# Grouped feed-forward: when the expert weights are split into a high and a low part

## The reference, cut to what matters

```python
scores = softmax(x @ gate_w.T)               # 16 experts
topk_w, topk_idx = top_k(scores, 4)
topk_w = topk_w / sum(topk_w)
cw = zeros((T, E)).at[arange(T)[:, None], topk_idx].add(topk_w)
def _mlp(x, wg, wu, wd):
    return silu(x @ wg.T) * (x @ wu.T) @ wd.T
for each expert e:  acc += cw[:, e] * _mlp(x, w_gate[e], w_up[e], w_down[e])   # width 176
y = acc + _mlp(x, sw_gate, sw_up, sw_down)                                      # shared, width 352
```

## Time and profile before

| what | us |
|---|---|
| median of the runs | 1494.38 |
| the profiled execution | 1495.86 |
| its span | 1494.1 |
| TensorE busy / VectorE busy / ScalarE busy / GpSimd busy | 1313.7 / 1039.1 / 851.1 / 849.9 |
| TensorE's granted clock, mean over the span | 0.949 |

### The profile page before, as it was taken

One profiled execution on the slowest core, in us unless ns is written; L12 is line 12 of the kernel. 1 busy time (PEld: TensorE's weight loads), 2 busy tenths in 40 slices (PEclk: granted clock), 3 DMA queues, 4 the chain that ended last, 5 costly groups with the idle time before them and its releaser, 6 DMA issues.

```text
span 1494.1 us, 28548 instructions
## 1 busy us (share of the span) xinstructions
PE 1313.7 (88%) x8106; PEld 1102.4 (74%) x8106; DVE 1039.1 (70%) x2544; ACT 851.1 (57%) x2102; POOL 849.9 (57%) x752
## 2 busy tenths in 40 slices
PE   6999999999978986759898999899999989978983
PEld 4888888888867974547777777677777769867882
DVE  5676666656677545338888888788888877677545
ACT  1444444454435542248787877677778875435542
POOL 3555555530424773257877878677877740434772
PEclk9999999999988998759999999999999999979996
DMA  3000000002334336121222222122221202335335
GB/s 116 26 26 27 26 25 25 16 18 63 122 127 155 104 101 225 46 53 33 64 58 70 48 68 60 46 52 68 61 58 44 57 1 77 121 117 169 103 103 184
DMA packets 52271, 110.72 MB, mean 74 GB/s; under 512 B 11616, under 2 KB 21408, under 8 KB 51872
## 3 DMA queue, kind: packets, MB, share of 16 engines
q1 hardware_dynamic: 40992, 82.22, 19.2%
q0 software_dynamic: 9024, 24.65, 5.4%
q10 hardware_dynamic: 2112, 2.10, 0.4%
HBM read 64.11 MB, written 15.47 MB: 53 GB/s over the span
## 4 chain that ended last, share of the span: by engine, by line
PE 38%; issue 21%; POOL 19%; DVE 12%; DMA 5%; ACT 3%; POOLq 0%; SPq 0%; DVEq 0%; ACTq 0%
PE ps L1465 25%; PE ps L1620 7%; POOL pb_odd L1105 4%; POOL yt L1105 3%; DMA raw_w<-in_wx 3%; PE ps L1830 2%; POOL rb L1090 2%; DVE rb L547 2%; POOL z L1105 2%; DVE x_res L858 2%; POOL pb_low L1105 2%; POOL xg L1044 1%; POOL ra L1094 1%; PE ps L1552 1%; POOL ybuf L1053 1%
## 5 line engine op out<-in xcount | busy, mean ns | idle before, releaser
L917 DVE TENSOR_TENSOR pt_lo<-ps,pt_hi 128x512 fp32r<-128x512 f32 (+3 forms) x384 | 205.4, 548 | 53.3 <-ACT pt_hi L1384 47.0
L1465 PE MATMUL ps<-kh,qh 128*128 128x512 f32 (+3 forms) x768 | 203.8, 375 | 20.7 <-DMA qh<-qt_hi 9.0
L1384 ACT CAST pt_hi<-ps 128x512 fp32r<-128x512 f32 (+3 forms) x384 | 178.5, 481 | 58.8 <-PE ps L1830 51.1
L902 DVE TENSOR_REDUCE nmb<-ps 128x1 f32<-128x1024 f32 (+7 forms) x256 | 191.7, 749 | 27.2 <-PE ps L1465 26.1
L1465 PEld LDWEIGHTS ps<-kh,qh 128*128 128x128 f32 x768 | 131.7, 195 | 43.7 <-issue 12.6
L1465 PE MATMUL ps<-pt_hi,vst 128*128 128x512 f32 (+3 forms) x384 | 156.0, 406 | 1.2 <-DVE ra L882 1.1
L1044 POOL DMA_INDIRECT xg<-zbuf,gidx x94 | 97.5, 1037 | 101.3 <-DVE sidx L762 30.3
L1465 PE MATMUL ps<-pt_lo,vst 128*128 128x512 f32 (+3 forms) x384 | 132.3, 348 | 0.0
L1182 ACT ACTIVATE pa<-sma,nmax 128x192 f32<-128x192 f32 x128 | 57.3, 449 | 129.4 <-DVE nmax L584 105.2
L1009 POOL TENSOR_TENSOR pa<-pa,rinv 128x384 f32<-128x384 f32 x64 | 52.9, 827 | 130.5 <-DVE rinv L592 130.5
L1465 PE MATMUL ps<-w_ex,gx_hi 128*128 x376 | 103.2, 357 | 18.5 <-issue 16.9
(11 more groups left out here) (225 smaller groups left out, 4168.2 us busy)
## 6 DMA issues: line engine op xcount, KB each, us to landing
raw_w<-in_wx SPq DMA_DIRECT2D x36, 608.0 KB, 4.0
rb<-raw SPq DMA_DIRECT2D x192, 64.0 KB, 2.0
yg<-ybuf SPq DMA_DIRECT2D x8, 1024.0 KB, 8.2
qh<-qt_hi SPq DMA_DIRECT2D x64, 128.0 KB, 2.3
qh<-qt_lo SPq DMA_DIRECT2D x64, 128.0 KB, 2.4
wa<-in_wa SPq DMA_DIRECT2D x16, 384.0 KB, 3.0
wb<-in_wb SPq DMA_DIRECT2D x8, 384.0 KB, 3.7
wo_a<-in_wo_a SPq DMA_DIRECT2D x16, 128.0 KB, 2.0
```

The source lines that it names most:

```text
L902: v.tensor_reduce(nmb[:, par, i:i + 1], ps[:, b:b + 2, :].rearrange("p b k -> p (b k)")[:, 0:P * (t + 1)], AX.X, ALU.max, negate=True).the ...
L917: v.tensor_tensor(pt_lo[:, s % 3, at], ps[:, 4 + s % 2, at], pt_hi[:, s % 3, at].bitcast(F32), ALU.subtract).then_inc(sem("b_pt_lo"), 1)
L1384: s_.copy(pt_hi[:, s % 3, at], ps[:, 4 + s % 2, at]).then_inc(sem("b_pt_hi"), 1)
L1465: return t_.matmul(o, l, r, start=start, stop=stop)
```

## The change

Only the two tables change. Before, two weights are converted in three steps: high part of one, then high part of the next together with the remainder of the first, then the remainder of the next. After, one weight is converted in two steps: its high part at the end of an even step on ScalarE, its remainder at the end of the odd step behind it on VectorE. Steps 0 to 3 stay.

```diff
-ACT_HI = {0: (2,), 1: (3,), 2: (4,), 3: (5,), 5: (6,), 7: (7,), 9: (8,), 10: (9,), 12: (10,), 13: (11,), 15: (12,), 16: (13,),
-          18: (14,), 19: (15,), 22: (16,), 23: (17,)}
-DVE_LO = {7: (6,), 8: (7,), 10: (8,), 11: (9,), 13: (10,), 14: (11,), 16: (12,), 17: (13,), 19: (14,), 20: (15,), 23: (16,), 24: (17,)}
+ACT_HI = {0: (2,), 1: (3,), 2: (4,), 3: (5,)}
+ACT_HI.update({6 + 2 * (n - POOL_LO): (n,) for n in range(POOL_LO, N_W)})
+DVE_LO = {7 + 2 * (n - POOL_LO): (n,) for n in range(POOL_LO, N_W)}
```

## The result

The changed kernel takes 1488.74 us (median of 8 runs, 1482.41 to 1492.39) beside 1494.95 for the kernel before (8 runs, 1490.80 to 1497.09): ratio 0.9953, 95% interval [0.9937, 0.9969]. Forecast: 1484, range 1479.5 to 1490.5. The change does what was said, and is worth about 7 us by the ratio (4.6 to 9.4 by its interval; the medians differ by 6.2), not 10.8.

A forecast was written before the change was run, and what follows sets the result against it. Each layer was paced by the routing table, then the split's load waits, then GpSimd; gains of 6.1 us in f and 4.7 in g, together 10.8, led from the runs' median to 1484 us, range 1479.5 to 1490.5.

The forecast's parts named there:

- the load wait: ScalarE's waits for raw weights in both feed-forward layers: 28.9 us before, forecast to fall under 17.
- one stall: Mixed stretch, TensorE at position 18: the only stall per four-step cycle, 1.3 us, behind a remainder on VectorE.
- the late weight: Weight 17's remainder, now in step 29, delays position 31's gate/up products: 2.4 us once per layer, bounds 0 and 3.3.
- GpSimd carries: Behind b=17, GpSimd's pace of 2.57 us per gather carries the gain to each layer's end.
- rival A: Part given back through a dearer routed stretch and last remainder, or TensorE's clock: gain 3 to 8 us, about 1489; chance 0.28.
- routed stretch: Steps 22 to 29 cost more than before: 5.46 us per weight against 4.24, bounds 5.15 and 6.2.
- b=17: GpSimd's gather of iteration 17, first behind the last remainder: forecast about 6 us earlier in f, 5 in g.
- first weights: Start of the split, up to G(15): 2.1 us earlier in f, 1.9 in g.
- G(15): TensorE's start of the gate/up products for position 15: forecast at 447.1 in f, 1343.8 in g.
- mixed stretch: Four-step cycle from G(15): forecast 9.3 us, against 12.4 in f and 11.7 in g before.
- tie with TensorE: At b=17 GpSimd's own path takes 36.1 us, TensorE's 36.25, so meeting remainders costs nothing.
- held gathers: GpSimd's dense stretch: four gathers per layer meet a remainder, taking 1.77 us instead of 0.97, 0.8 more each.

The follow-up runs named there:

- e10: The changed kernel once more, unaltered, on one chip with e11: 1488.79 us, 0.9954 of the kernel before.
- e2: Kernel before (old order), loading only the first quarter of each raw weight from number 8 on: 1483.69 us, 0.9922 of the kernel before.
- e3: Changed kernel, loading only the first quarter of each raw weight from number 8 on: 1487.11 us, 0.9934 of the kernel before.
- e5: Changed kernel, each remainder's large instruction taking its first input from PSUM instead of the raw weight: 1487.58 us, 0.9949 of the kernel before.
- e6: Changed kernel with both e4's order and e5's PSUM input: 1481.49 us, 0.9912 of the kernel before.
- e9: Changed kernel with indirect scatters replaced by plain SyncE stores, GpSimd only gathering: 1472.46 us, 0.985 of the kernel before.
- e4: Changed kernel with weights 14 to 17 in pairs again (high parts in steps 22, 23, 25, 26): 1486.19 us, 0.9939 of the kernel before.
- e1: The changed kernel again, no edit: 1487.22 us, 0.9948 of the kernel before.
- e8: Kernel before (old order) with indirect scatters replaced by plain SyncE stores, GpSimd only gathering: 1479.32 us, 0.9892 of the kernel before.
- e7: Changed kernel with weights 6 to 8 converted in steps 5 to 7, last remainder in step 25: 1483.34 us, 0.9919 of the kernel before.
- e11: e7's order once more, unaltered, on one chip with e10: 1482.58 us, 0.9922 of the kernel before.

## Why the prediction was right, and where its size was off

The time, 1488.74, lies inside the range, and the mechanism is the one forecast: the load wait goes, one stall is left, the late weight costs, GpSimd carries. But the gain, 6 to 7 us, is below the forecast's own band of 8 to 13.5 and in that of rival A, 3 to 8, whose two causes (a dearer routed stretch, TensorE's clock) both turned up in part. Of the signs named, the one on b=17, about 6 and 5 us earlier, failed in size: it was 3.9 and 4.0.

Each term as forecast and as measured, us gained, from the layer's first gather:

| term | forecast | after | e10 |
|---|---|---|---|
| first weights, f: G(15) | 2.1 | 0.5 | 0.5 |
| first weights, g | 1.9 | 2.1 | 2.2 |
| mixed stretch, f: G(15) to G(19) | 3.1 | 3.2 | 3.2 |
| mixed stretch, g | 2.4 | 2.5 | 2.5 |
| G(19) to b=17, f | 0.9 | 0.2 | 0.2 |
| G(19) to b=17, g | 0.4 | -0.6 | -0.2 |
| sum at b=17 | 10.8 | 7.8 | 8.3 |
| sum at the end | 10.8 | 6.4 | 7.8 |

**The load wait and the mixed stretch: right.** Walked 9.3, measured 9.22 in both layers, with the one stall at position 18 where it was put (in f X(19) 6.37 after G(15) for 6.3, G(18) 7.34 for 7.25). The waits for raw weights fell to 14.4 us, below the 17 named. e2 shows the cause: short loads alone bring the old order to 9.4.

**First weights: right in g, a quarter in f.** This is the largest miss, 1.6 us. In the profiles after, TensorE is granted the lower of its two levels (1.2 instead of 2.4 GHz) in f's first positions behind the first gather; before, it was not. Busy time and granted clock (the column behind the five engines) of 430 to 440 us, before and then after, and of 460 to 470 after, which answers to the earlier trace rows:

```profile
430.00:440.00 10.00, 6.80 (x46) 6.11 (x46) 6.50 (x17) 4.26 (x10) 5.35 (x6) 0.99 0.64 201
```

```profile
430.00:440.00 10.00, 7.61 (x35) 6.64 (x34) 5.22 (x15) 3.48 (x8) 6.08 (x6) 0.67 0.46 142
...
460.00:470.00 10.00, 9.17 (x62) 8.00 (x61) 7.96 (x21) 6.58 (x17) 5.34 (x5) 1.00 0.61 196
```

35 instructions in 7.61 us of busy time, where before 46 took 6.80. G(10), a pair of products that takes 0.58 at the full clock:

```profile
436.79 0.95 PE L1465 MATMUL ps<-w_ex,gx_hi 128*128 x2 [0.47 <-issue]
```

From G(10) to G(12) it takes 5.4 us in f, and 3.7 in g, where the full clock is back 6 us behind the first gather, just before G(10). Over the profiles of the new order, unaltered or with one edit, G(15) of f goes with the moment at which the granted clock is back at the higher level, both in us from the first gather: back at 6.0 to 6.4, G(15) at 17.6 to 18.5 (e3, e5, e6, e9); back at 8.9 and 9.1, G(15) at 19.4 and 19.1 (e4, e1); back at 10.9 and 11.6, G(15) at 19.8 and 19.9 (the first profile after, e10). My walk assumed 2.4 GHz throughout and put it at 18.2. So the clock is what the term left out, though no run changes the clock alone. Why it is late in f is open. In the old order it is back at 1.3 and 1.6 (before, e2) but at 8.9 in e8, so the lower clock isn't the new order's doing alone; in all ten profiles that spread the conversions (e7 and e11 too) it is back only at 6.0 or later. Whether the new order makes it likelier, so few profiles don't tell. The lower clock that I had named for 460 to 470 (rival A) is gone there, as the walk said.

**The routed stretch and weight 17: right in kind, 0.7 and 1.1 us too short.** In f, G(19) to G(24) is 12.95 for 12.7, G(24) to G(30) 16.57 for 16.4, G(30) to G(31) 4.90 for 4.6; X(33) and the gather follow in 1.89 and 0.65 as walked: 36.96 for 36.25. In g one place is worse: G(24) to G(26) takes 5.82 instead of 5.5, with an idle of 0.91 (5.48 in e10, so not in every execution). Here rival A was partly true, at a quarter to a third of the 3.1 per layer given for it. In e1, e3 and e5 the idle 2.7 ahead of G(31) is followed by products at the lower clock (0.93 to 0.95 us for a pair that takes 0.58): the clock's share of rival A exists, but not in every execution.

**GpSimd: the pace right, its tie with TensorE right in kind, the size and number of held gathers wrong.** I took 1.77 for each of four; there are nine long ones per layer, of 1.31 to 1.73, so 0.3 to 0.8 more each; of those from b=8 on in f, five, none is over 1.41, and they sum to 1.9 for the 3.2 of my walk. The trace says why they are shorter. b=8 of f starts at 469.04, when this remainder has run for 0.6 us:

```profile
468.44 1.15 DVE L768 TENSOR_TENSOR w_ex<-raw_w,w_ex 128x960 fp32r<-128x960 f32 x1
```

Each long gather or scatter ends some 0.84 us after the remainder it met, so what it loses is what was left of the remainder: with 0.2 us gone it takes 1.77, as before, and with 0.6 gone 1.4. One that had started before the remainder isn't held (1.00 us for the scatters of f that do). That this is the remainder's doing was read from the trace, and e5 shows it: with one input in PSUM all nine are gone. The Trainium skill, page "SBUF — State Buffer", section "Who interferes with whom", has a rule that fits this, that a VectorE instruction with two SBUF inputs contends with a GpSimd instruction that reads SBUF, and one with at most one SBUF input, outside the two-port modes, doesn't. The same section's inference that a tensor_tensor leaves descriptor generation alone doesn't hold in these runs. That it "costs nothing" in the new order is right as well, to within what e5 can tell. The cover is thin: GpSimd was ready 1.54 us before TensorE in f and 0.25 in g, where the walk had 0.15, and in g it is that thin only by the gap ahead of iteration 9, which the walk didn't have.

**Behind b=17: 1:1, less up to 0.8 per layer.** The sum at the end is 0.5 to 1.4 below that at b=17. From b=17 to the last gather it takes 64.2 us in both layers, before and after, so up to there nothing is lost. Behind it the last block's gate and up products start 7.7 / 6.8 after the last gather before, 8.5 / 7.7 after and 8.0 / 7.1 in e10; in f TensorE stands 1.30 there for gathered rows to land, where it stood 0.34 before. Why they land later is open. The reason given was too narrow: the carrying doesn't need GpSimd's pace (e9).

## What to carry to other kernels

When a double buffer is refilled by a load of several microseconds, spread its uses evenly: from one release every two steps, each load has the same time to land, where bunched uses waited for the slow ones. Then look at both ends of the schedule. An even pace ends later, and its last item gated a block for 2.6 us; running two weights ahead, by starting in a window where the engines wait anyway, was worth 4 to 6 us more, beside the 7 of the change. And where two engines tie, an edit of either alone can measure nothing: test the pair, and compare where each engine stands, since such an edit can also bring an old wait back, as e4 did.

## What the runs showed that I had not expected

- A VectorE subtraction of 1.15 us with both inputs in SBUF holds a gather or scatter that GpSimd starts while it runs, until some 0.84 us after its end: 1.3 to 1.8 us instead of 0.97 and 0.99. One that GpSimd had started before is not held, and with one input in PSUM, at the same 1.15 us, none is.
- A stretch that no edit touches (layer b, 740 us) differs by 4.3 us between three profiles of one kernel (738.8 to 743.1: e1, e10, after), and by 5.3 over all profiles here, so spans of two profiles don't measure an effect of this size.
- The moment at which TensorE's full clock is back behind the first gather of f lies between 6.0 and 11.6 us in ten profiles of nearly the same order, and goes with a G(15) up to 2 us later.
